# A decoder layer on one core: the last tile's projection in two column parts, and four stretches of the work in another order

## What is computed

```python
x = x + attn(layernorm(x), ...)          # 8 heads of a fixed memory M, z: elu(q)+1, num/den, times Wo
x = x + xattn(layernorm(x), ctx, ...)    # softmax attention, 32 query heads, 4 key/value heads
x = x + ffn(layernorm(x), ...)           # 64 experts, top 8, bias mix

# xattn, per batch row
q = latents @ Wq                         # 512 -> 32*128
k, v = [context; latents] @ Wk, @ Wv     # 512 -> 4*128
out = softmax(q k^T / sqrt(128)) v @ Wo  # 4096 -> 512

# ffn
logits = flat @ router.T + bias ; scores = softmax(logits)
w, idx = top_k(scores, 8) ; out = flat * w.sum() + dense(w, idx) @ expert_bias
```

## Time and profile before

| what | before |
|---|---|
| median of 3 runs | 699.23 us (699.2 to 699.68) |
| the profiled execution, its own time | 699.29 us |
| its span, first to last instruction | 697.5 us |
| mean granted TensorE clock | 0.996 of full speed |
| busy: PE / PEld / DVE / ACT / POOL | 99% / 83% / 75% / 50% / 19% |

### The profile page before, as it was taken

The page is one execution under the profiler, slowest core; times in us unless marked ns, Lnnn a source line. Parts: engine busy times, 40 slices in busy tenths (PEclk is TensorE's granted clock), DMA queues, the critical chain, the costliest instruction groups (busy, mean ns, idle before and its releaser), DMA issues.

```text
span 697.5 us, 11041 instructions
## 1 busy us (share of the span) xinstructions
PE 687.2 (99%) x3560; PEld 579.3 (83%) x3560; DVE 520.5 (75%) x1098; ACT 351.1 (50%) x1047; POOL 133.8 (19%) x136
## 2 busy tenths in 40 slices
PE   8999999999999999999999999999999999999996
PEld 7888888888878788888888888888888888788884
DVE  3774966778877888677678876767877657878887
ACT  4454845455443454454346643555635435755543
POOL 0296000000512232022020220210202000322321
PEclk9999999999999999999999999999999999999998
DMA  9996240001325557433342733423643414231101
GB/s 329 371 351 245 67 145 1 1 0 46 121 76 193 184 160 251 142 122 106 107 152 68 233 105 105 150 84 103 191 143 113 141 41 129 77 115 61 46 32 60
DMA packets 70605, 90.14 MB, mean 129 GB/s; under 512 B 4192, under 2 KB 48480, under 8 KB 70560
## 3 DMA queue, kind: packets, MB, share of 16 engines
q1 hardware_dynamic: 65632, 81.71, 35.7%
q10 hardware_dynamic: 4928, 7.87, 3.1%
HBM read 62.29 MB, written 27.26 MB: 128 GB/s over the span
## 4 chain that ended last, share of the span: by engine, by line
PE 93%; DVE 3%; ACT 2%; POOL 1%; issue 1%; ACTq 0%; DVEq 0%; POOLq 0%
PE bank L978 24%; PE bank L907 23%; PE bank L727 13%; PE bank L1091 8%; PE bank L881 6%; PE bank L1147 6%; PE bank L1121 4%; PE bank L718 2%; PE bank L1047 1%; PE bank L846 1%; PE bank L768 1%; PE bank L812 1%; DVE forms L1566 1%; PE bank L802 1%; PE bank L750 0%
## 5 line engine op out<-in xcount | busy, mean ns | idle before, releaser
L978 PE MATMUL bank<-regA,oT 128*128 128x512 f32 x762 | 180.2, 391 | 0.2 <-DVE oT L1566 0.2
L978 PEld LDWEIGHTS bank<-regA,oT 128*128 128x128 f32 x762 | 142.0, 188 | 29.6 <-DVE oT L1566 0.4
L1474 ACT ACTIVATE probs<-bank,negmax 128x128 f32<-128x128 f32 x256 | 89.9, 377 | 42.8 <-DVE negmax L2007 42.8
L907 PE MATMUL bank<-xnT,forms 128*128 128x512 f32 x432 | 108.8, 396 | 0.5 <-DVE qbuf L1776 0.4
L907 PEld LDWEIGHTS bank<-xnT,forms 128*128 128x128 f32 x432 | 79.0, 188 | 17.6 <-DVE qbuf L1776 1.9
L907 PE MATMUL bank<-regC,forms 128*128 128x512 f32 x324 | 83.8, 397 | 1.6 <-DVE qbuf L1776 0.9
L1181 ACT CAST oT<-bank 128x512 fp32r<-128x512 f32 (+1 forms) x66 | 37.7, 573 | 79.5 <-PE bank L1147 76.5
L907 PEld LDWEIGHTS bank<-regC,forms 128*128 128x128 f32 x324 | 59.0, 188 | 13.4 <-DVE regC L1566 1.3
L1181 ACT CAST pT<-bank 128x512 fp32r<-128x512 f32 x64 | 34.6, 593 | 66.9 <-PE bank L1121 66.7
L727 PE MATMUL bank<-regC,xnT 128*128 128x512 f32 x256 | 68.0, 396 | 0.0
L648 POOL TENSOR_TENSOR diff<-wq_raw 128x256 f32<-128x256 f32 x17 | 13.4, 786 | 283.3 <-DVE forms L1566 283.3
(11 more groups left out here) (195 smaller groups left out, 1058.8 us busy)
## 6 DMA issues: line engine op xcount, KB each, us to landing
q_dram<-qbuf SPq DMA_DIRECT2D x32, 512.0 KB, 3.2
qbuf<-q_dram SPq DMA_DIRECT2D x31, 512.0 KB, 4.8
raw<-in_L_xattn_Wo SPq DMA_DIRECT2D x4, 2048.0 KB, 10.5
wq_raw<-in_L_xattn_Wq SPq DMA_DIRECT2D x16, 512.0 KB, 4.1
raw<-in_L_attn_Wo SPq DMA_DIRECT2D x6, 1024.0 KB, 8.9
k_ring<-keys_dram SPq DMA_DIRECT2D x32, 128.0 KB, 3.5
v_raw<-vals_dram SPq DMA_DIRECT2D x64, 64.0 KB, 3.4
resid<-in_x SPq DMA_DIRECT2D x4, 512.0 KB, 11.6
```

What stands on the lines that cost most here:

```text
L907: last = nc.tensor.matmul(k_bank[:, :], forms[:, p[1], a, i, c, :], right(b)[:, c, :], start=j == 0, stop=j == 5)
L978: last = nc.tensor.matmul(bank[7][:, :], oT[:, a, h, :], wo[:, b, h, :], start=h == 0 and i == 0, stop=h == GH - 1 and i == 2)
L1474: last = nc.scalar.activation(probs[:, bb, p, :], bank[bb][:, p * P:(p + 1) * P], ACT.Exp, bias=negmax[:, bb, p:p + 1], accum_out=rowsum[: ...
```

## The change

The changed parts, by place. **Start:** `spin(3)` becomes `spin(1)`; chunks 0 and 1 of tile 1 get the early rule too; the transposes of tiles 2 and 3 come one chunk earlier. **Key stage:** vlat 7 goes to bank 0, product 6 of pair 0 no longer waits for its copy; on ACT `t_high(1)` and `t_high(2)` stand ahead of that copy, and S2 of pair 1 behind `t_high(3)`; on DVE the first sums change places (`sum_11` ahead of `sum_u2`), `t_low(2)` and `t_low(3)` move up, and for every pair S2's low (`inner_low`) stands behind `sum_21`. **Steps 24 and 25:** POOL makes three lows of Wo (heads 3 to 5) in place of four, DVE heads 6 and 7 in step 25, around the softmax. **End:** heads 2 and 3 close bank 7, heads 4 to 7 go into banks 1 and 0 with 256 columns each; DVE adds three times; `save_last_xn` stands ahead of `scale_rows(6)`; the last tile's maximum comes from a reduce with a sign; 12 transposes of the identity stand ahead of the last expert weights.

```diff
@@ mm_bank
+            if (kind, i) == ("vlat", NT - 1):
+                return bank[0]
@@ POOL
-            for h in range(4, GH):
+            for h in range(3, GH - 2):
@@ TensorE, start
-            spin(3)
+            spin(1)
...
-                if (t, c) == (0, 3):
+                if (t, c) == (1, 2):
                     context_transposes(1)
-                early = t == 0 and c < 2
+                early = c < 2
@@ TensorE, key stage
+                if t == NT - 1:
+                    pe.wait_ge(tr_used, tr("latent", NT - 2) + 1)
...
             def product_4(p):
-                pe.wait_ge(q_summed, 7 * p[0] + 2)
+                pe.wait_ge(q_summed, 7 * p[0] + 2 if follows(p[0], 1) else 1)
...
             def product_5(p):
+                if not follows(p[0], 1):
+                    pe.wait_ge(q_summed, 2)
...
                 if p == 0:
-                    pe.wait_ge(mm_act, mm_act_count(mm("vlat", 7)))
                     pe.wait_ge(sig_lo, 2 * NT)
@@ TensorE, end
+            def project_columns(half):
+                for h in range(GH // 2, GH):
+                    for i, (a, b) in enumerate(PARTS):
+                        last = nc.tensor.matmul(bank[1 - half][:, 0:D // 2], oT[:, a, h, :],
+                                                wo[:, b, h, half * (D // 2):(half + 1) * (D // 2)],
+                                                start=h == GH // 2 and i == 0, stop=h == GH - 1 and i == 2)
+                last.then_inc(proj_done, 1)
...
+            for h in range(2, GH // 2):
+                for i, (a, b) in enumerate(PARTS):
+                    last = nc.tensor.matmul(bank[7][:, :], oT[:, a, h, :], wo[:, b, h, :], start=False,
+                                            stop=h == GH // 2 - 1 and i == 2)
+            last.then_inc(proj_done, 1)
             pe.wait_ge(oT_lo, 2 * KV * NT + 2)
-            project(KV - 1, NT - 1, False, range(2, 5))
+            project_columns(0)
             expert_weights(NT - 3)
-            project(KV - 1, NT - 1, False, range(5, GH))
+            project_columns(1)
...
             expert_mix(NT - 2)
+            spin(12)
             expert_weights(NT - 1)
@@ ACT
                 if t == 6:
-                    summed_high(1, 1)
+                    outer_high(1, 1)
+            act.wait_ge(mm_done, mm("vlat", NT - 1) + 1)
             t_high(1)
+            t_high(2)
+            save_latent_values(NT - 1)
             for p in range(LEAD + 1):
-                if p == 0:
-                    t_high(2)
                 copy_1(p)
                 if p == 0:
                     t_high(3)
+                    inner_high(1, 1)
...
+            save_last_xn()
             scale_rows(NT - 2)
-            save_last_xn()
@@ DVE, key stage
-            summed_low(1, 1)
+            outer_low(1, 1)
             t_low(1)
+            t_low(2)
             for p in range(LEAD + 1):
                 if p:
                     direct_low(p + 1, (p + 1) % 2)
+                if p == 0:
+                    sum_11(p)
                 sum_u2(p)
                 if p == 0:
-                    t_low(2)
-                if p < LEAD:
+                    t_low(3)
+                elif p < LEAD:
                     sum_11(p)
-                if p == 0:
-                    t_low(3)
                 if p < LEAD:
                     if p:
-                        summed_low(p + 1, (p + 1) % 2)
+                        outer_low(p + 1, (p + 1) % 2)
                     sum_u3(p)
                     sum_21(p)
+                    inner_low(p + 1, (p + 1) % 2)
                     sum_22(p)
@@ DVE, steps 24 and 25
+                if last_group and t == 1:
+                    dve.wait_ge(wo_lo, GH * (KV - 1) + GH - 2)
+                    wo_low(KV - 1, GH - 2)
...
+                if last_group and t == 1:
+                    wo_low(KV - 1, GH - 1)
...
-                    for h in range(2, 4):
+                    for h in range(2, 3 if p is None else 4):
                         wo_low(g, h)
@@ DVE, end
+                if e == NT - 1:
+                    nc.vector.tensor_reduce(top[:, r, 1, 0:1], logits, axis=AX, op=ALU.max, negate=True)\
+                        .then_inc(e_max_ready, 1)
+                    settled(nc.vector.max(top[:, r, 0, :], logits))
...
+            def add_columns(half):
+                dve.wait_ge(proj_done, KV * NT + 1 + half)
+                rows = resid[:, NT - 1, half * (D // 2):(half + 1) * (D // 2)]
+                nc.vector.tensor_tensor(rows, rows, bank[1 - half][:, 0:D // 2], ALU.add).then_inc(proj_added, 1)
...
             expert_max(NT - 2)
+            dve.wait_ge(proj_done, KV * NT)
+            settled(nc.vector.tensor_tensor(resid[:, NT - 1, :], resid[:, NT - 1, :], bank[7][:, :], ALU.add))
             add_mix(NT - 4)
             raw_weights_of(NT - 2)
+            add_columns(0)
             row_factors(NT - 2)
-            dve.wait_ge(proj_done, KV * NT)
-            for half in range(2):
...
+            add_columns(1)
```

More of the change, by code:

```diff
@@ L1081, in step @@
                 if first_step:
+                    pe.wait_ge(mm_act, mm_act_count(mm("vlat", NT - 1)))
                     pe.wait_ge(tr_used, tr("latent", NT - 1) + 1)
@@ L1209, in summed_high, with inner_high @@
                 high(form_dst(slot, 0, S1), raw_pair(p, 1)).then_inc(form_hi, 1)
+            def inner_high(p, slot):
                 act.wait_ge(form_summed, 4 * p + 4)
                 high(form_dst(slot, 0, S2), raw_pair(p, 0)).then_inc(form_hi, 1)
+            def summed_high(p, slot):
+                outer_high(p, slot)
+                inner_high(p, slot)
             def copy_1(p):
@@ L1378, in t_high @@
                 high(t_block((T2, 3, T4, T1)[r], 0), sums[:, (1, 2, 3, 0)[r], :, :]).then_inc(t_hi, 1)
-            for t in range(NT):
+            for t in range(NT - 1):
                 save_latent_values(t)
@@ L1926, in expert_max @@
                                                            in1=rout_b, op0=ALU.mult, op1=ALU.add))
-                settled(nc.vector.max(top[:, r, 0, :], logits))
-                nc.vector.tensor_scalar(top[:, r, 1, 0:1], top[:, r, 0, 0:1], -1.0, None, ALU.mult)\
-                    .then_inc(e_max_ready, 1)
+                if e == NT - 1:
+                    nc.vector.tensor_reduce(top[:, r, 1, 0:1], logits, axis=AX, op=ALU.max, negate=True)\
+                        .then_inc(e_max_ready, 1)
+                    settled(nc.vector.max(top[:, r, 0, :], logits))
+                else:
+                    settled(nc.vector.max(top[:, r, 0, :], logits))
+                    nc.vector.tensor_scalar(top[:, r, 1, 0:1], top[:, r, 0, 0:1], -1.0, None, ALU.mult)\
+                        .then_inc(e_max_ready, 1)
                 nc.vector.match_replace(rest, top[:, r, 0, :], logits, TAKEN).then_inc(e_rest_ready, 1)
@@ L2092, in _ @@
                 step(KV - 1, t, True)
+            def add_columns(half):
+                dve.wait_ge(proj_done, KV * NT + 1 + half)
+                rows = resid[:, NT - 1, half * (D // 2):(half + 1) * (D // 2)]
+                nc.vector.tensor_tensor(rows, rows, bank[1 - half][:, 0:D // 2], ALU.add).then_inc(proj_added, 1)
             expert_max(NT - 2)
+            dve.wait_ge(proj_done, KV * NT)
+            settled(nc.vector.tensor_tensor(resid[:, NT - 1, :], resid[:, NT - 1, :], bank[7][:, :], ALU.add))
             add_mix(NT - 4)
             raw_weights_of(NT - 2)
+            add_columns(0)
             row_factors(NT - 2)
-            dve.wait_ge(proj_done, KV * NT)
-            for half in range(2):
-                rows = resid[:, NT - 1, half * (D // 2):(half + 1) * (D // 2)]
-                nc.vector.tensor_tensor(rows, rows, bank[7][:, half * (D // 2):(half + 1) * (D // 2)], ALU.add)\
-                    .then_inc(proj_added, 1)
+            add_columns(1)
             dve.wait_ge(proj_added, 8 * KV + 2)
```

11 lines of the change are left out of this document (8 added, 3 removed).

## The result

| what | before | after |
|---|---|---|
| median | 699.38 us (699.20 to 700.18, 7 runs) | 701.84 us (700.74 to 702.85, 7 runs) |
| ratio after / before | | 1.0035, 95% interval 1.0025 to 1.0044 |
| the profiled execution, span | 699.29 us, 697.5 us | 701.36 us, 699.6 us |
| mean granted TensorE clock | 0.996 | 0.999 |

A forecast was written before the change was run, and what follows sets the result against it. TensorE, busy 687.2 of 697.5 us, was taken as the bound, so only its waits could be won; -0.55 (start) - 2.1 (key stage) + 0 (lead loop) + 0.2 (steps 24 and 25) - 0.2 (end) = -2.65 on 699.29: 696.6, range 695.2 to 698.5.

The forecast's parts named there:

- Start: Kernel start: early rule and fewer spins end the wait for tile 1's low context; gain 0.55, bounds 0 to 0.7.
- Key stage: Pair 0's products: product 4 starts at 196.3 without waiting, not 198.48; gain 2.1, bounds 1.3 to 2.2.
- the walk: The prediction's instruction-by-instruction retiming of the new orders, using durations and clock of the trace before; key stage gain 2.1.
- Lead loop: Pairs 2 to 5: S2's later low shortens TensorE's wait but delays loads; 0, bounds gain 1.1, loss 1.5.
- The first step: After the lead loop's last pair: `copy_1` 1.5 later, first softmax 0.8 later, which may cost 0.25.
- Steps 24 and 25: Lows of Wo: new router wait of 0.4 to 0.7 replaces the old; loss 0.2, bounds gain 0.4, loss 1.1.
- End: Last tiles, bounded by DVE: third add costs, reduce and clock-holding transposes gain; gain 0.2, bounds gain 0.7, loss 0.8.
- Rival 6: Lead loop: weight load meets the store behind it and lands late; 1.2 late costs 4.4, giving 701.0; chance 0.03.
- Rival 3: Lead loop: later load shows fully through `direct_high` ahead of `copy_1`, 0.4 on four pairs, 698.2; chance 0.14.

The follow-up runs named there:

- e4: Changed kernel with each lead-loop weight load from pair 3 on cut to its first half (256 of 512 KB); 696.88 us, ratio 0.9961.
- e2: Kernel before with one change: S2's low behind `sum_21` for pairs 1 to 5; 703.29 us, ratio 1.0057.
- e6: Kernel before with only the part of steps 24 and 25 (POOL heads 3 to 5, DVE heads 6 and 7); 699.37 us, ratio 1.0001.
- e9: Kernel before with only the twelve transposes ahead of the last tile's expert weights; 699.30 us, ratio 1.0001.
- e7: Kernel before with only the whole end part (column parts, twelve transposes, maximum by reduce, ACT's order); 699.55 us, ratio 1.0.
- e3: Changed kernel with ACT's `direct_high` behind `copy_1` and DVE's direct low behind `sum_u2` in the lead loop; 701.34 us, ratio 1.0029.
- e5: Changed kernel with the lead loop's four query stores cut to a quarter, buffer filled ahead by copies; 708.04 us, unusable because those copies held up other transfers.

## Why the prediction was wrong

The forecast was 696.6 (695.2 to 698.5), the result 701.84: outside the range and on the other side. The step that failed is the lead loop, its period "about 9.9 us" and its price: "I count the loop at 0; bounds a gain of 1.1 ... and a loss of 1.5".

- **Start**: -0.55 forecast, -0.26 at tile 2's values and -0.17 by product 1 in this pair of traces. Over all of them tile 2 starts at 12.96 to 13.66 in the ten with the part (this one at 13.04) and at 13.08 to 13.61 in the six without it (the kernel before at 13.30), so even these 0.2 us can't be told from the scatter of the first loads. The wait for tile 1's low parts went; part of what replaced it is the data, 0.36 us for tile 1, which the two spins taken away had covered. The lower bound, 0, was the nearer one.
- **Key stage**: -2.1 forecast, -2.25 measured. Each link came within 0.3 us of the walk; two waits are left, both of weight loads, 0.22 for product 5, the link that the walk had as its tightest, and 0.16 for product 3. The mechanism was right here.
- **Lead loop**: 0 forecast with "about 9.9" for the period, 2.77 lost at 10.6. The walk saw what decides, that the next load comes later, and asked what a late load holds up. It did not ask what the late load meets. It took the landing of 3.8 and POOL's sums of 0.74 over from the trace of before. But once SP is released late, the pair's store is already due and goes out 0.42 us behind the load: 0.5 more of landing in each period. The order itself adds some 0.26. The bound of 1.5, 0.4 on each of four pairs, rested on the same durations.
- **The first step**: 0.25 forecast ("may cost 0.25"), 1.44 measured. It is the same loop's last round: the load of 251.11 holds up the direct forms on ACT and DVE, and with them the first softmax. e4 shows it: with a landing of 2.8 us the stretch loses 0.05.
- **Steps 24 and 25**: +0.2 forecast, +0.4 measured. The new wait is there as put (0.36 for "0.4 to 0.7"); the old one hardly shrank (0.37, before 0.44). POOL's three lows ended as the walk had them (604.75, which is 602.9 on the clock of before), but step 25's second probabilities, 0.69 us when alone, took 1.15 from 606.41 on, beside a low v that POOL had begun at 606.28, and so were ready at 607.56, 605.74 on the clock of before, where the walk had 605.4 to 605.7.
- **End**: -0.2 forecast, -0.1 to -0.2 measured, the sum about right, in part by luck: the column parts cost 0.5 and not 0.2, the reduce and ACT's order gave 0.4 and not 0.2, and the gain of 0.2 for the transposes is the difference of two traces that e2's and e6's traces have without them. DVE bounds the end, as put, and the last add then waits for `scale_rows`. The rule of the Trainium skill on transposes and the clock, weighed in the prediction, does not fit e9's mean clocks, 0.998 to 1.000 in eleven runs against 0.996 to 0.998, nor e7's recovery. The start, on which the prediction rested its doubt, could not tell: the granted clock stands at 1.00 there before the first transpose. Nor does 0.47 us for one transpose compare with 0.66 for a record of four; one takes 0.33 at full rate.

**The rivals.** Rival 6 had the mechanism: "the weight load, which now meets the store that SP issues right behind it, lands late. Beyond about 0.1 us every us of landing is a us on each of four periods". At the measured 0.5 late its own rule gives 4 x 0.4 = 1.6 of the 2.77; the order's 0.26 a period brings it to 2.6, and the first step comes on top. It had 0.03, on the argument that "the load is ahead of the store in its queue". Being ahead didn't protect it: with 0.42 us between them both are in flight for most of the 4.3 us. Rival 3 named a place, `direct_high` ahead of `copy_1`, and e3 shows that place to be no cause. The text's own test, "wrong if a lead pair lasts over 10.2 us", struck.

What stays open: how the order's 0.26 a period divides between DVE's queue and POOL's stretched sum; why a store of a quarter of the size still does more than half of the harm; and what decides whether the clock falls before the last transposes.

## What to carry to other kernels

A loop that runs from a load over other engines to the next load is a bound of its own: write down its period beside TensorE's, and where it is already the longer of the two, as here (9.89 against 9.65), treat every delay of its issue as a loss. When an edit moves the issue of a transfer, look in the DMA queue's timeline for what is issued next to it before and after, and price the landing by that neighbour and not by the old landing. And before trusting a bundle of small reorderings, run the bundle with its riskiest line taken back: here one line turned -2.3 us into +2.5.

## What the runs showed of the hardware

- A 512 KB load lands in 3.7 to 3.8 us (medians of five or six) with a store of the same size 1.2 to 1.4 us behind it, in 4.2 to 4.3 with the store 0.4 to 0.6 us behind, and in 4.1 with one of 128 KB 0.42 us behind (e5); being first in SP's queue doesn't protect it.
- With twelve 128x128 transposes in the gap, the mean clock is 0.998 to 1.000 in e9's eleven runs, against 0.996 to 0.998 before, and in e7 the clock came back from 0.51 while nothing else ran. Started at the lower level they cost 2.70 us and not 1.47, so filling a gap with them is a bet: worth at most 0.2 us in e9's trace, and 1.3 us lost in e7's (27.38 against 26.08). The gaps ahead of it were the same in e7 and in the changed kernel (0.52 and 0.28 us).
- Where a DVE instruction with two operands in SBUF and one of POOL meet, the later one stretches, whichever it is: POOL's sum from 0.74 to 1.07 us (changed kernel, 237.83), DVE's low from 0.42 to 0.90 (kernel before, 246.64, POOL's sum from 246.52), the probabilities from 0.69 to 1.15 (changed kernel, 606.41).
- In a run of LDWEIGHTS and 256-column matmuls the pitch stays at half that of 512 columns: in the changed kernel the twelve of a half start at 686.32 and the next twelve at 687.78, with the transpose of an expert weight between them, 1.46 us beside 1.38 for six of 512 columns, so column parts cost TensorE next to nothing. Their cost is on the engine that adds.
